# Attention scores from source products that hold the query weights, in a graph network on one Trainium2 core

## The reference

```python
def _transformer_conv(x, src, dst, edge_attr, wq, bq, wk, bk, wv, bv, we, ws, bs, n_nodes):
    q = x @ wq + bq
    k = x @ wk + bk
    v = x @ wv + bv
    e = edge_attr @ we
    ke = k[src] + e
    score = jnp.sum(q[dst] * ke, axis=-1) / jnp.sqrt(...)
    ...                      # softmax over the edges of one destination: alpha
    msg = alpha[:, None] * (v[src] + e)
    out = jax.ops.segment_sum(msg, dst, num_segments=n_nodes)
    return out + x @ ws + bs
```

## Time and profile before

| what | us |
|---|---|
| median of three runs | 6880.25 |
| profiled execution | 6867.82 |
| its span | 6865.4 |
| first pass, first gather to last read of psY | 2779.49 to 3600.49 |
| second pass, the same | 4016.28 to 4824.59 |
| busy in the whole span: TensorE, VectorE, ScalarE, GpSimd | 4521.3, 4547.4, 1784.2, 3994.9 |
| mean granted clock of TensorE, share of full | 0.849 |

### The profile page before, as it was taken

One profiled execution on the slowest core, in us unless ns is written; L12 is line 12 of the kernel. 1 busy time (PEld: TensorE's weight loads), 2 busy tenths in 40 slices (PEclk: granted clock), 3 DMA queues, 4 the chain that ended last, 5 costly groups with the idle time before them and its releaser, 6 DMA issues. The chain is left out here.

```text
span 6865.4 us, 102108 instructions
## 1 busy us (share of the span) xinstructions
PE 4521.3 (66%) x31726; PEld 4063.2 (59%) x31726; DVE 4547.4 (66%) x5826; ACT 1784.2 (26%) x2462; POOL 3994.9 (58%) x3348
## 2 busy tenths in 40 slices
PE   6665345770188788466766857777587856875897
PEld 3454335660177787466665856766587755764675
DVE  7898553225677788699989833333887965772458
ACT  5543112330044344233323411111343420000001
POOL 0397765771277678777765877775000027757756
PEclk9766668995598999688778979999899978997999
DMA  6498766668855477333335844444477861221109
GB/s 234 108 275 257 154 149 140 141 133 321 339 174 166 136 243 251 78 96 99 101 84 184 265 125 136 131 131 125 149 254 281 312 244 41 56 91 50 14 11 299
DMA packets 865606, 1128.70 MB, mean 164 GB/s; under 512 B 591583, under 2 KB 604276, under 8 KB 864060
## 3 DMA queue, kind: packets, MB, share of 16 engines
q1 hardware_dynamic: 409660, 807.13, 35.3%
q10 hardware_dynamic: 311296, 226.11, 10.8%
q0 software_dynamic: 144256, 90.12, 9.0%
HBM read 633.88 MB, written 495.44 MB: 164 GB/s over the span
## 5 line engine op out<-in xcount | busy, mean ns | idle before, releaser
L895 POOL DMA_INDIRECT gc_msgs<-t,src_rows x784 | 754.4, 962 | 1131.5 <-POOLq L148 837.3
L2005 PEld LDWEIGHTS gc_ring<-gc_msgs,gc_hot 128*128 128x128 f32 x4736 | 621.6, 208 | 310.4 <-issue 303.6
L2005 PE MATMUL gc_ring<-gc_msgs,gc_hot 128*128 x4736 | 648.8, 295 | 234.1 <-SPq L1964 233.0
L949 POOL DMA_INDIRECT acc<-de_sums,de_put x392 | 607.5, 1550 | 307.7 <-issue 146.6
L895 POOL DMA_INDIRECT edge_rows<-x,dst_rows x392 | 508.4, 1297 | 164.9 <-issue 117.1
L895 POOL DMA_INDIRECT edge_rows<-h,dst_rows x392 | 479.5, 1223 | 210.5 <-issue 117.3
L895 POOL DMA_INDIRECT re_rows<-x,src_rows x392 | 406.2, 1036 | 125.3 <-issue 124.7
L895 POOL DMA_INDIRECT at1s_ends<-x,src_rows x392 | 395.6, 1009 | 128.8 <-issue 119.2
L895 POOL DMA_INDIRECT at2s_ends<-h,src_rows x392 | 372.3, 950 | 134.7 <-issue 118.2
L1477 PE MATMUL re_psR<-w_rel,re_own 128*128 128x128 f32 x3136 | 396.9, 292 | 70.9 <-DVE re_own L1414 70.4
L1477 PEld LDWEIGHTS re_psR<-w_rel,re_own 128*128 128x128 f32 x3136 | 389.6, 208 | 80.1 <-issue 77.1
(11 more groups left out here) (491 smaller groups left out, 11718.9 us busy)
## 6 DMA issues: line engine op xcount, KB each, us to landing
rew_win<-x SPq DMA_DIRECT2D x74, 544.0 KB, 4.8
at1w_win<-g SPq DMA_DIRECT2D x74, 544.0 KB
at2w_win<-g SPq DMA_DIRECT2D x74, 544.0 KB, 4.1
de_win<-t ACTq DMA_DIRECT2D x74, 512.0 KB, 4.6
de_near<-same SPq DMA_DIRECT2D x74, 512.0 KB, 5.0
x<-rew_win SPq DMA_DIRECT2D x74, 512.0 KB
h<-at1w_win SPq DMA_DIRECT2D x74, 512.0 KB
h<-at2w_win SPq DMA_DIRECT2D x74, 512.0 KB, 2.9
```

The source lines that it names most:

```text
L895: nc.gpsimd.indirect_dma_start(buf[:, t * width:(t + 1) * width], None, table, bass.IndirectOffsetOnAxis(ap=rows[:, t:t + 1], axis=0)).the ...
L949: nc.gpsimd.indirect_dma_start(g.acc0[j % LANES], bass.IndirectOffsetOnAxis(ap=put[:, j:j + 1], axis=0), sums[:, j * D:(j + 1) * D], None, ...
L2005: done = nc.tensor.matmul(ring[:, bass.ds(to[n], SLOT)], hot[k][:, n, :], each_group(msgs[:, bass.ds(of[n], MID)], SLOT // MID), start=Fal ...
```

## The change

The score of an edge is the product of q[dst] and ke. Since q is linear in the destination row h, the sum over q can be drawn into the other factor: q . ke = h . (Wq ke) + bq . ke. The new kernel folds the query weights into the key weights once ahead of each pass (`lay_out` on VectorE, six products on TensorE). For an edge it then computes one vector u = Wq (k + e) of 64 values, the message v + e, and one number bq . ke, all from the source row and the attributes, in one group of 258 columns for two tiles: 128 of u, 128 of v, 2 of the number. The biases come in by a row of ones under the turned attributes, so a product over 65 rows holds them. The destination rows are no longer turned or multiplied with weights; VectorE multiplies them with u out of PSUM (L1718, maximum with zero included), and adds up. In the first pass the factor of the layer norm of a destination row is applied to its 8 sums (L1722) and no longer to its 512 values. ScalarE copies the message and the number out of PSUM (`keep`), which VectorE did with the bias. The wait for the destination rows moves from `turn` to the dot product (first pass: it stays in `centre`). In the second pass the two dense products share one weight tile of 256 columns, and a piece is 2 such products.

AHEAD is 24 in both kernels, and the merge stages and the gathers are not touched.

```diff
-        psS, psD, psE, psQ, psK, psV, psX, psY = (r.ps(n, [P, 512]) for n in (...))
+        psS, psE, psX, psY = (r.ps(n, [P, 512]) for n in ("psS", "psE", "psX", "psY"))
+        psU = r.ps("psU", [P, B // 2, 512])
...
             def inputs_ready(eng, b):
                 eng.wait_ge(got[b.slot], 16 * B * b.nth)
-                eng.wait_ge(ahead[b.slot], 16 * B * b.nth)
                 eng.wait_ge(ea_in[b.slot], 32 * b.nth)
...
@@ turn, TensorE
                     transpose_pairs(nc, psS, ends[s], g.ident, B // 2)
                     for k in range(B // 2):
-                        nc.tensor.transpose(psD[:, k * P:(k + 1) * P], values[:, b.number * W + k * P:b.number * W + (k + 1) * P], g.ident[:, :])
-                    transpose_pairs(nc, psE, ea[s % 2], g.ident, B // 4)
-                    transpose_pairs(nc, psX, x[:, 0:W], g.ident, B // 2).then_inc(turned, 1)
+                        nc.tensor.transpose(psE[0:D, k * P:(k + 1) * P], ea[s % 2][:, k * D:(k + 1) * D], g.ident[:, :])
+                    transpose_pairs(nc, psX, xd[s % 2][:, 0:W], g.ident, B // 2).then_inc(turned, 1)
@@ project, TensorE
-                    times(nc, psQ, hdT[s % 2], wq, B // 2)
-                    for to, w in ((psK, wk), (psV, wv)):
-                        for h in range(2):
-                            nc.tensor.matmul(to[:, h * 256:(h + 1) * 256], eaT[s % 2][:, h * P:(h + 1) * P], we[:, :], start=True, stop=False,
...
+                    for j in range(B // 2):
+                        nc.tensor.matmul(psU[:, j, 0:PUT], eaT[s % 2][0:D + 1, j * P:(j + 1) * P], from_attr[:, :], start=True, stop=False,
+                                         skip_group_check=True)
+                        last = nc.tensor.matmul(psU[:, j, 0:PUT], hsT[s % 2][:, j * P:(j + 1) * P], from_src[:, :], start=False, stop=True,
+                                                skip_group_check=True)
@@ ScalarE
-                    nc.scalar.activation(hdT[s % 2][:, :], psD[:, :], ACT.Relu)
-                    nc.scalar.activation(eaT[s % 2][:, :], psE[:, 0:B * DE], ACT.Copy)
+                    nc.scalar.activation(eaT[s % 2][0:D, :], psE[0:D, :], ACT.Copy)
...
+                def keep(b):
+                    act.wait_ge(dotted, b.number + 1)
+                    nc.scalar.activation(grouped(far(b), P), psU[:, :, P:2 * P], ACT.Copy)
+                    nc.scalar.activation(grouped(scores[:, bass.ds(b.number * B, B)], 2), psU[:, :, 2 * P:PUT], ACT.Copy).then_inc(used, 1)
@@ VectorE
-                    nc.vector.tensor_tensor(grouped(far(b), D), grouped(far(b), D), spread(root[:, 0, B:J], D), ALU.mult)
...
+                def dot(b):
+                    if not normalise:
+                        dve.wait_ge(ahead[b.slot], 16 * B * b.nth)
+                    dve.wait_ge(product, b.number + 1)
+                    nc.vector.scalar_tensor_tensor(grouped(dots[:, :], P), grouped(far(b), P), 0.0, psU[:, :, 0:P], ALU.max, ALU.mult).then_inc(dotted, 1)
+                    dve.wait_ge(dotted, b.number + 1)
+                    link(nc.vector.tensor_reduce(found[:, :], grouped(dots[:, :], D), AXX, ALU.add))
+                    if normalise:
+                        link(nc.vector.tensor_tensor(found[:, :], found[:, :], sd[b.slot % 2][:, 0, B:J], ALU.mult))
+
                 def score(b):
-                    nc.vector.tensor_tensor(grouped(q[:, :], D), grouped(psQ[:, :], D), each_group(bq[:, :], B), ALU.add)
-                    nc.vector.tensor_tensor(grouped(values[:, bass.ds(b.number * W, W)], D), grouped(psV[:, :], D), each_group(bv[:, :], B), ALU.add)
-                    nc.vector.tensor_tensor(grouped(k_[:, :], D), grouped(psK[:, :], D), each_group(bk[:, :], B), ALU.add).then_inc(used, 1)
+                    at = scores[:, bass.ds(b.number * B, B)]
                     dve.wait_ge(used, b.number + 1)
-                    link(nc.vector.tensor_tensor(q[:, :], q[:, :], k_[:, :], ALU.mult))
-                    link(nc.vector.tensor_reduce(scores[:, bass.ds(b.number * B, B)], grouped(q[:, :], D), AXX, ALU.add))
+                    link(nc.vector.tensor_tensor(at, at, found[:, :], ALU.add))
```

More of the change, by code:

```diff
@@ L1507, in attention_scores @@
     bq, bk, bv = (g.w[n] for n in biases)
-    pieces = [(h, n) for n in range(len(dense)) for h in range(2)]
-    M = len(pieces)
+    N2 = len(dense)
+    EACH = 4 // N2
+    M = J // 2 // EACH
+    PUT = 2 * P + 2
     with Room(nc, g, name + "s") as r:
@@ L1513, in attention_scores @@
         ea = [r.sb(f"ea{k}", [P, B * DE]) for k in range(2)]
[L1514 to L1516 removed]
+        outs = [r.sb(f"outs{k}", [P, N2 * C]) for k in range(2)]
+        hsT, eaT, xT = ([r.sb(f"{n}{k}", [P, w]) for k in range(2)] for n, w in (("hsT", W), ("eaT", W), ("xT", C)))
+        dots, found = g.zeros[:, 0:W], g.zeros[:, W:W + B]
+        from_src, from_attr = r.sb("from_src", [P, PUT]), r.sb("from_attr", [D + 1, PUT])
+        key_rows, query_bias = r.sb("key_rows", [D + 1, P]), r.sb("query_bias", [P, P])
+        own_w = g.w[dense[0][0]] if N2 == 1 else r.sb("own_w", [P, N2 * P])
+        own_b = r.sb("own_b", [P, N2, 2, D])
+        tipped_w = xT[0]
+        KEY, ATTR, QUERY, BIAS = 0, P, 2 * P, 3 * P
         if normalise:
@@ L1604, in stage @@
                         for m in some:
-                            h, n = pieces[m]
                             if not (isinstance(b.number, int) and b.number == 0 and m == 0):
                                 pe.wait_ge(piece_read, b.number * M + m)
-                            times(nc, psY, xT[s % 2][:, h * W:(h + 1) * W], g.w[dense[n][0]], B // 2).then_inc(piece, 1)
+                            times(nc, psY, xT[s % 2][:, m * EACH * P:(m + 1) * EACH * P], own_w, EACH).then_inc(piece, 1)
                     return stage
@@ L1649, in _, with lay_out @@
                 link = Link(dve, link_s)
+                def lay_out():
+                    v = nc.vector
+                    v.tensor_copy(key_rows[0:D, :], we[0:D, 0:P])
+                    v.tensor_copy(grouped(key_rows[D:D + 1, :], D), each_group(bk[D:D + 1, :], 2))
+                    v.tensor_copy(grouped(query_bias[:, :], D), each_group(bq[:, :], 2)).then_inc(laid, 1)
+                    for k in range(2):
+                        v.memset(eaT[k][D:D + 1, :], 1.0)
+                    for n, (_, bias, _) in enumerate(dense):
+                        v.tensor_copy(own_b[:, n, :, :], each_group(g.w[bias][:, :], 2))
+                        if N2 > 1:
+                            v.tensor_copy(own_w[:, n * P:(n + 1) * P], g.w[dense[n][0]][:, :])
+                    v.tensor_copy(from_src[:, P:2 * P], wv[:, :])
+                    v.tensor_copy(from_attr[0:D, P:2 * P], we[0:D, 0:P])
+                    v.tensor_copy(grouped(from_attr[D:D + 1, P:2 * P], D), each_group(bv[D:D + 1, :], 2))
+                    link(v.memset(tipped_w[:, BIAS:BIAS + 2], 0.0))
+                    dve.wait_ge(tipped, 1)
+                    v.tensor_copy(tipped_w[:, 0:ATTR + D + 1], psS[:, 0:ATTR + D + 1])
+                    v.tensor_copy(tipped_w[:, QUERY:QUERY + P], psS[:, QUERY:QUERY + P])
+                    v.tensor_copy(tipped_w[0:D, BIAS:BIAS + 1], psS[0:D, BIAS:BIAS + 1])
+                    v.tensor_copy(tipped_w[D:P, BIAS + 1:BIAS + 2], psS[D:P, BIAS:BIAS + 1]).then_inc(folded, 1)
+                    dve.wait_ge(combined, 1)
+                    for to, ps in ((from_src[:, :], psX[:, :]), (from_attr[:, :], psY[0:D + 1, :])):
+                        v.tensor_copy(to[:, 0:P], ps[:, 0:P])
+                        last = v.tensor_copy(to[:, 2 * P:PUT], ps[:, P:P + 2])
+                    last.then_inc(weights_made, 1)
                 def centre(b):
@@ L1688, in stage @@
                         for m in some:
-                            h, n = pieces[m]
                             dve.wait_ge(piece, b.number * M + (m + 1))
-                            nc.vector.tensor_tensor(grouped(outs[n][s][:, h * W:(h + 1) * W], D), grouped(psY[:, :], D),
-                                                    each_group(g.w[dense[n][1]][:, :], B), ALU.add).then_inc(piece_read, 1)
+                            to = outs[s][:, :].rearrange("p (n q w) -> p q n w", n=N2, w=P)[:, m * EACH:(m + 1) * EACH]
+                            nc.vector.tensor_tensor(to, psY[:, :].rearrange("p (q n w) -> p q n w", n=N2, w=P),
+                                                    own_b[:, :, :, :].rearrange("p n u d -> p n (u d)").unsqueeze(1).to_broadcast([P, EACH, N2, P]),
+                                                    ALU.add).then_inc(piece_read, 1)
                     return stage
+                lay_out()
                 if normalise:
-                    pipeline(dve, order=[(1, variance), (1, scale), (2, score), (2, take(0)), (0, centre), (2, take(1))], slots=SLOTS)
+                    pipeline(dve, order=[(1, variance), (1, scale), (2, dot), (2, take(0)), (2, score), (0, centre), (2, take(1))], slots=SLOTS)
                 else:
```

(2 more changed lines are left out.)

32 lines of the change are left out of this document (17 added, 15 removed).

## The result

The changed kernel takes 6824.08 us (median of 4 runs, 6807.53 to 6830.23), the kernel before 6881.99 in the same runs: ratio 0.9918, 95% interval 0.9905 to 0.9931. The prediction was 6812, range 6788 to 6850; the forecast gain was 68 us, the medians differ by 58 and the two profiled executions (6867.82 and 6807.53) by 60.3. Later runs of the kernel before, made beside the experiments, have medians of 6867 to 6873; so the experiments' whole times are compared by their ratio to the kernel before, and their passes by the profiles.

What follows compares the result with a forecast made beforehand. VectorE was taken to bound pass one, with GpSimd's gathers 1.0 us behind, and a TensorE-VectorE relay pass two. Gains of 11 + 57 = 68 us gave 6812 by the runs' median, range 6788 to 6850.

Steps and rivals of the forecast that it cites:

- Gathers as the common floor: GpSimd, both passes: 1.248 us from gather to gather, 737.6 us for 591 spaces, no step under 14.98 us.
- Pass two, 57 us: Second pass: gathers become the bound in place of the TensorE-VectorE relay; end at 4767.8 against 4824.6, 57 us gained.
- The relay's step: TensorE and VectorE in pass two: step falls from 16.48 to 13.6 us, under the gathers' 14.98.
- Pass one, 11 us: First pass: 7.5 us from fewer slowed gathers (42 lost against 49.5) plus 3.6 at its end, 11 gained.
- the term of L1711 and L1712: Pass one: in every step a gather meets one of these two-input VectorE instructions and loses about 0.50 us, 49 times.
- The term of the three L748: Pass one: steps whose centring starts on a landing lose 0.27, 0.30 and 0.14 us under L748, 24 x 0.71.
- The 3.6 us at the end of the pass: Pass one's last step, all in series: less scaling, product, transposes, evacuation and score chain shorten it by 3.6 us.
- VectorE's 14.1 us a step: Pass one: 4.24 us removed against 2.36 added leave VectorE 14.1 us a step, under 14.98, so GpSimd becomes the bound.
- the best case of 86: Both passes: only 24 us of collisions in pass one and 60 gained in pass two, 86 in all: 6794 us.
- Even odds in pass one: Rival: no lock forms, gathers start evenly spread; pass one loses 72 us where it lost 49.5; 6842, chance 0.15.
- The slow clock of TensorE: Rival, pass two: TensorE stays the bound below clock 0.73; 6900 and more, chance 0.05; half the gain, 6850, 0.07.
- The new handover through ScalarE: Rival, pass two: VectorE's dot, ScalarE's copy, TensorE's next product replace the removed chain, adding 2.9 us a step; 6870, chance 0.03.

Runs made afterwards that it cites:

- pass one without pairs: Changed kernel, layer norm's five two-input tensor_tensor instructions in pass one replaced by equally long one-input reductions (rows not normalised): 6753.97 us, pass one 768.2.
- second_only: Old scores in the first pass, new ones in the second: 6814.01 us, ratio to the kernel before 0.992; pass two 750.4.
- first_only: New scores in the first pass alone, old ones in the second: 6871.38 us, ratio to the kernel before 1.0001; pass one 821.5.
- no_pair: Layer norm's two-input tensor_tensor instructions replaced by equally long reductions in pass one: kernel before 6866.58 us (pass one 821.5), changed kernel 6753.97 (768.2).
- factors_in_psum: Changed kernel with pass one's layer norm means and factors in PSUM and attributes turned later: 6758.05 us, ratio to the kernel before 0.984.
- pair_in_two: Changed kernel plus two idle 512-element additions on two SBUF inputs in each step of pass two: 6804.34 us, pass two 760.0.
- reduce_in_two: Changed kernel plus two idle equally long one-input reductions in each step of pass two: 6802.71 us, pass two 750.2.

## Why the prediction was right, and where it was off

**Gathers as the common floor.** 591 x 1.248 = 737.6 us was forecast; pass two has 737.8, and pass one without pairs 737.8 (2778.93 to 3516.77). Held exactly; in five kernels pass two has 737.8 to 738.0.

**Pass two, 57 us.** 56.2 in the profiled pair, 58 with `second_only` (808.3 to 750.4). The end was forecast 751.5 us after the first gather and came at 752.1. The relay's step was forecast at 13.6, of it 11.8 at full clock and 1.8 of work at the lower one. Measured is 11.66 in the step at a clock of 1.00 and 13.3, without its wait, in the one that has 0.50 after waiting for rows: the carried-over 1.8 us come back there and not in every step. It makes no difference, since the gathers' 14.98 lie above both.

**Pass one, 11 us.** This is the step that failed in size: "A step whose centring starts on the landing of its last gather meets three L748 with 0.27, 0.30 and 0.14 us; every step meets L1668 or L1670 with about 0.50. Sum 42 us." The last gather began 786.6 us after the first, so 49.0 were lost, and 49 to 53 in the four profiles that have the new pass one whole, with its two-input instructions unchanged (49.0, 49.4, 50.2 and 53.4 with 592 gathers). Gathers over 1.00 us rose from 98 to 132, though two of seven two-input instructions are gone. Told apart by what VectorE runs when a gather begins, the term of L1711 and L1712 (L1668 and L1670 before) was forecast at 24.5 us and is 22.0. The term of the three L748 is the mis-sized one: 17 forecast, 27 measured. In the steps that wait for a landing they cost 15; in the 23 others, where I had put them at nothing, 12. I had laid one pattern of starts over the step and taken it for all; hits like that at 3299.34, worth 1.02 at once, are not in it. The size before was no guide either: there VectorE set the pace and GpSimd lost what it was ahead, 46 times under L1668 and 46 under L1670. That nothing holds the phase where it is cheap once VectorE follows is my explanation and was not tested. The 3.6 us at the end of the pass were 5.0 (25.2 us from landing to end in place of 30.2). Together 5.7 in this profile, 1.6 to 2.3 in two others with the same pass one (818.7 and 819.4), none in `first_only`: the true gain of pass one is about 2 us with a spread of 3.

**VectorE's 14.1 us a step.** 14.10. The mechanism that turned on it (the bound moves to GpSimd) is shown by the pair of `no_pair` runs.

**Three readings.** I took the extra 0.51 and 0.49 us of rows 3 for the time left of the VectorE instruction. What was left was 0.63 and 0.61, and every slow gather loses 0.11 to 0.13 less than what is left. Rows 3 also show no gather that begins under L1675 or L1691; the trace has them, 47 under L1691 and 43 under L1676, another PSUM reader, in pass one, 21 under L1675 in pass two, and none is slow. And the best case of 86 leaves out the 3.6 us at the end of pass one: it is 89.

**The rivals.** Even odds in pass one (72 us lost) and my pattern (42) lie on both sides of the measured 49 to 53. With the holds as measured, 0.52 and 1.05 us in place of 0.60 and 1.14, the even-odds sum is 59 (an estimate), so the measured loss lies between the pattern and the even odds. The slow clock of TensorE came in part: 0.88 for 0.93 in pass two, where 0.73 would have decided, and 0.78 for 0.82 in pass one; in `factors_in_psum` pass one has 0.73 and is the fastest. The rule of the Trainium skill, "TensorE: Matmul & The Clock Gate" under "HAM oscillation — how this bites in real kernels", that short bursts between waits for data start cold agrees with the 0.50 after the wait of 5.16 us. It cost nothing here, since TensorE was not the bound. The new handover through ScalarE never showed: its two copies (0.60 and 0.17, from 4503.04) ended 6 us before the next product. The folding of weights took 6.0 us on VectorE in pass two (7 forecast) and was done 5.4 us after the first gather began; the pass used its first gathered rows 11.2 us after that start.

**The sum.** 68 forecast, 60.3 in the profiled pair, 58 by medians. Of the missing 8 in the profiled pair, 5 are pass one, 1 pass two, the rest is drift in stages with unchanged code. Nothing here tells where the last 2 us between profiled pair and medians come from; the runs of one kernel spread by some 20.

## What to carry to other kernels

When an engine's queue has no wait but "issue", multiply its count by the start-to-start time: that floor is the next bound as soon as the present one falls below it, however low its busy share. A loss on an engine that is not the bound (49 us of slow gathers) costs nothing, until a change makes this engine the bound; then it counts (47 us here), so look for it among what you leave in place. Test it with an instruction of equal length that lacks only the suspected property, in the kernel before and in the kernel after.

## What the runs showed of the hardware

A gather by index on GpSimd's queue that starts while VectorE runs a float32 instruction of 512 or 1024 elements with two SBUF inputs waits for its end: 0.94 us become up to 1.46 under 512 elements and up to 2.00 under 1024. An equally long reduction (one input) and a product whose second input lies in PSUM did not slow one gather. Which access of the gather waits, no run here separates.

The order of the two starts decides, but not to the nanosecond. In the traces of five kernels (before, changed, `first_only`, `pair_in_two`, `reduce_in_two`) the 708 slow gathers all began 0.044 us or more after the VectorE instruction. The 60 that began up to 0.044 us after it were not slow; there the VectorE instruction got longer, as this one, which else takes 1.22:

```profile
3313.29 1.30 DVE L748 TENSOR_TENSOR at1s_xd<-at1s_xd,at1s_sums 128x1024 f32<-128x1024 f32 x1
3313.33 0.94 POOL L895 DMA_INDIRECT edge_rows<-x,dst_rows  x1 [0.30 <-issue]
```

So the other way the loss is small: at most 0.08 us. L1711 has a median of 708 ns in the changed kernel, against 692 for the same form before; it is 0.69 where the gather begins 0.1 us behind it and 0.70 to 0.72 where the gather begins just ahead. The Trainium skill, "SBUF — State Buffer" under "SBUF: two separate sides", has whoever starts first hold the pair of ports for its whole instruction. For VectorE's side the 708 rows agree, apart from those first 0.044 us; for the gather's they do not, since no gather held VectorE for its 0.94 us. So a gather seems to take the shared access only for a short part of its time.
